# Layer ends of a five-layer graph network: unit 48 a step sooner, unit 49's kept parts ahead of the last sum, maps stored in smaller pieces

## The reference, cut to what matters

```python
edge_index = jnp.stack([src, dst])                       # dst sorted
x = _layernorm(x + _L0(x, edge_index, ...))              # sum x[src]; elu MLP 64->256->64
x = _layernorm(x + _L1(x, src, dst, edge_attr_32, ...))  # MLP per edge, sum, MLP per node
x = _layernorm(x + _L2(x, edge_index, ...))              # SAGE mean, batch norm, SAGE mean, x added
x = _layernorm(x + _L3(x, weight, src, dst, edge_type))  # x[src] @ weight[type], summed
```

## Time and profile before

| | |
|---|---|
| median of 3 runs | 9928.48 us (9926.42 to 9930.86) |
| the profiled execution's own time | 9929.83 us |
| its span, first to last instruction | 9928.0 us |
| busy share of the span | POOL 74%, PE 51%, PE weight loads 43%, DVE 26%, ACT 13% |
| gathers | 5 x 1,563 |
| mean granted TensorE clock | 0.583 of full speed |

### The profile page before, as it was taken

One profiled execution on the slowest core, in us unless ns is written; L12 is line 12 of the kernel. 1 busy time (PEld: TensorE's weight loads), 2 busy tenths in 40 slices (PEclk: granted clock), 3 DMA queues, 4 the chain that ended last, 5 costly groups with the idle time before them and its releaser, 6 DMA issues.

```text
span 9928.0 us, 68540 instructions
## 1 busy us (share of the span) xinstructions
PE 5057.8 (51%) x23622; PEld 4285.6 (43%) x23623; DVE 2602.1 (26%) x5963; ACT 1280.8 (13%) x2646; POOL 7381.4 (74%) x7823
## 2 busy tenths in 40 slices
PE   4555555566666666344444445666666633323333
PEld 3444444456666666333333334444555422222222
DVE  2222222233444443111111113333333311111111
ACT  1111111111111111000000001222222200000000
POOL 7777777767777777677777777777777667777777
PEclk6555555577777777555555555555555555555555
DMA  3111111133333333111111112222222211111111
GB/s 73 33 33 34 33 33 34 32 88 92 93 93 93 93 93 87 27 30 30 30 30 30 30 29 68 78 78 81 79 79 80 76 29 28 28 28 29 28 28 28
DMA packets 396618, 525.10 MB, mean 53 GB/s; under 512 B 175674, under 2 KB 232868, under 8 KB 396200
## 3 DMA queue, kind: packets, MB, share of 16 engines
q0 software_dynamic: 250080, 359.01, 16.0%
q1 hardware_dynamic: 56929, 81.63, 2.8%
q10 hardware_dynamic: 89255, 80.01, 2.6%
HBM read 442.81 MB, written 77.29 MB: 52 GB/s over the span
## 4 chain that ended last, share of the span: by engine, by line
POOL 74%; issue 25%; PE 1%; DVE 0%; DMA 0%; ACT 0%; ACTq 0%; POOLq 0%; DVEq 0%
POOL G L436 74%; PE PAG L1095 0%; PE NB L1095 0%; PE NA L1095 0%; PE PH L1095 0%; DMA G<-in_x,SRC 0%; DMA near_tab<-STG 0%; DVE FA L715 0%; DMA G<-rel_tab,IDX 0%; DMA h_tab<-STG 0%; ACT L503 0%; DMA G<-far_tab,SRC 0%; DMA G<-h_tab,SRC 0%; DVE HT L1031 0%; DMA G<-x_tab,SRC 0%
## 5 line engine op out<-in xcount | busy, mean ns | idle before, releaser
L1095 PE MATMUL PAG<-OH,G 128*64 128x96 f32 (+2 forms) x12544 | 2369.8, 383 | 3844.0 <-DMA G<-rel_tab,IDX 1370.1
L1095 PEld LDWEIGHTS PAG<-OH,G 128*64 128x64 f32 (+2 forms) x12544 | 2167.4, 253 | 4094.6 <-issue 3623.9
L436 POOL DMA_INDIRECT G<-rel_tab,IDX x1563 | 1474.7, 944 | 525.5 <-issue 525.5
L436 POOL DMA_INDIRECT G<-far_tab,SRC x1563 | 1474.9, 944 | 515.6 <-issue 476.1
L436 POOL DMA_INDIRECT G<-x_tab,SRC x1563 | 1475.5, 944 | 503.3 <-issue 476.0
L436 POOL DMA_INDIRECT G<-h_tab,SRC x1563 | 1475.0, 944 | 498.0 <-issue 475.7
L436 POOL DMA_INDIRECT G<-in_x,SRC x1563 | 1479.0, 946 | 476.1 <-issue 475.2
L779 DVE TENSOR_TENSOR AGG<-AGG,PAG 64x96 f32 (+2 forms) x980 | 245.6, 251 | 5510.9 <-PE PAG L1095 5501.0
L1095 PE MATMUL PAG<-OH,HT 128*128 128x96 f32 x3136 | 652.6, 393 | 630.2 <-ACT HT L614 630.2
L748 DVE TENSOR_TENSOR OH<-CONST,DREL 128x768 f32<-128x768 f32 x981 | 927.9, 946 | 3.7 <-issue 2.7
L1095 PEld LDWEIGHTS PAG<-OH,HT 128*128 128x128 f32 x3136 | 607.3, 297 | 678.0 <-ACT HT L614 677.6
(11 more groups left out here) (151 smaller groups left out, 3840.1 us busy)
## 6 DMA issues: line engine op xcount, KB each, us to landing
rel_tab<-STG ACTq DMA_DIRECT2D x100, 500.0 KB
HT<-dst_rows SPq DMA_DIRECT2D x196, 192.0 KB
HT<-in_efT SPq DMA_DIRECT2D x196, 128.0 KB
G<-in_x,SRC POOLq DMA_INDIRECT x1563
G<-far_tab,SRC POOLq DMA_INDIRECT x1563
G<-x_tab,SRC POOLq DMA_INDIRECT x1563
G<-h_tab,SRC POOLq DMA_INDIRECT x1563
G<-rel_tab,IDX POOLq DMA_INDIRECT x1563
```

What stands on the lines that cost most here:

```text
L436: pool.indirect_dma_start(out=G[:, h, j, 0:tabs[p].shape[1]], out_offset=None, in_=tabs[p], in_offset=bass.IndirectOffsetOnAxis(ap=numbers ...
L1095: return nc.tensor.matmul(dst, lhsT, rhs, start=start, stop=stop, skip_group_check=True)
```

## The change

- `SEGMENTS` and `straight_schedule`: unit 47 begins in step 188 and unit 48 in step 192, one step sooner than before; from unit 47 on a stage after the first may share a step with the stage before it. Unit 48 now ends in step 194, step 195 has no stage, and only unit 49 is left after the last step.
- `fetch` is cut in two. `keep` copies what doesn't depend on the sums (`XU`, `IU`, in layer 3 the relu of `HT`); for unit 49 it runs in step 195, ahead of the last sum. `take_sums` copies `Z` and clears `AGG`. In layer 0 `keep` also runs a one-element exp, so that the table for exp is loaded there.
- On PE the matmuls of biases and of kept parts come ahead of those that need `Z`; for unit 49 they are issued ahead of step 195's sum (`last_unit_early`). The degree goes to `PH` after the hidden products.
- The last step's sum, its mixing add and its relu and shift work on 3 chunks in place of 8.
- Layer 0's maps: the far map goes to `NA`, is copied and stored by itself and has its own semaphore, `far_stored`, for which POOL waits; the near map (with the bias) follows through `NB`. SP still waits for the near map.
- Layer 3's maps are stored in four transfers of 125 x 512 a unit in place of two of 125 x 1024.
- The one-hot matrices of the next layer's step 0 are made after unit 49; the bias row is stored without its zero half; the prologue has one more small operation (a fourth segment).

```diff
-SEGMENTS = [(0, 25, 5), (25, 40, 3), (40, UNITS - 1, 1)]
+SEGMENTS = [(0, 25, 5), (25, 40, 3), (40, UNITS - 3, 1), (UNITS - 3, UNITS - 1, 0)]
...
-            if begins[u] > s or (now and begins[u] + stage > s):
+            quick = stage > 0 and u >= SEGMENTS[-1][0]
+            if begins[u] > s or (now and begins[u] + stage - quick > s):
...
+def filled_chunks(s):
+    return max(1, min(GROUP, FILLED - s * GROUP))
...
-        STORE = [32, 16, 16, 32, 16]
+        STORE = [16, 16, 16, 64, 16]
...
                 if p == 1:
-                    pool.wait_ge(stored[0], all_stored(0))
+                    pool.wait_ge(far_stored, all_stored(0))
...
-                copy(Z[0:m, :], AGG[0:m, bass.ds(u * UNIT, UNIT)])
+            def keep(p, u):
+                if p == 0:
+                    nc.scalar.activation(WARM[:, :], ZERO[0:1, 0:1], ACT.Exp)
                 if p in (2, 3):
                     copy(IU[0:HALF, :], INV[0:HALF, bass.ds(u * 2, 2)])
...
+            def take_sums(p, u):
+                m = (D + 1, H, D, H, D)[p]
+                copy(Z[0:m, :], AGG[0:m, bass.ds(u * UNIT, UNIT)]).then_inc(staged[p], 1)
                 act.wait_ge(staged[p], u + 1)
                 act.sem_inc(act_go, 1)
                 copy(AGG[:, bass.ds(u * UNIT, UNIT)], ZERO[:, :]).then_inc(cleared[p], 1)
...
-                    act.wait_ge(l0_maps, u + 1)
-                    nc.scalar.activation(STG[0:HALF, :, 0:2 * H], NA[0:HALF, :].rearrange("p (a c) -> p a c", a=2),
-                                         ACT.Copy).then_inc(l0_maps_copied, 1)
...
+                    maps = [(l0_far, NA, 0, far_tab, far_stored), (l0_near, NB, H, near_tab, stored[0])]
+                    for k, (ready, bank, c, tab, landed) in enumerate(maps):
+                        act.wait_ge(ready, u + 1)
+                        nc.scalar.activation(STG[0:HALF, :, c:c + H],
+                                             bank[0:HALF, 0:2 * H].rearrange("p (a c) -> p a c", a=2), ACT.Copy)\
+                            .then_inc(l0_maps_copied, 1)
+                        act.wait_ge(l0_maps_copied, u * 2 + (k + 1))
+                        act.dma_start(rows_of(tab, u), STG[0:HALF, :, c:c + H]).then_inc(landed, 16)
...
+                    for k in range(4):
+                        a, b = k // 2, k % 2
+                        c = slice(b * 512, b * 512 + 512)
+                        act.wait_ge(l3_map, u * 4 + (k + 1))
+                        nc.scalar.activation(STG[0:HALF, a, c], PH[a][0:HALF, c], ACT.Copy).then_inc(l3_map_copied, 1)
+                        act.wait_ge(l3_map_copied, u * 4 + (k + 1))
+                        act.dma_start(rows_[a, b], STG[0:HALF, a, c]).then_inc(stored[3], 16)
...
+                        if s == SUPERS - 1:
+                            keep(p, LAST)
+                            if p in (1, 2):
+                                node[p](LAST, 1)
...
                     act.wait_ge(added, SUPERS * (p + 1) + 2)
-                    for u, stage in LATE:
-                        node[p](u, stage)
+                    take_sums(p, LAST)
+                    for stage in (2, 3) if p in (1, 2) else (1, 2, 3):
+                        node[p](LAST, stage)
...
-                for j in range(GROUP):
-                    last = mm(PAG[0:m, 0:WIN], msg[:, j, 0:m], OH[:, h % 2, j, :], j == 0, j == GROUP - 1)
+                for j in range(chunks):
+                    last = mm(PAG[0:m, 0:WIN], msg[:, j, 0:m], OH[:, h % 2, j, :], j == 0, j == chunks - 1)
...
+            def last_unit_early(p):
+                if p in (0, 3):
+                    node[p](LAST, 1, (0,))
+                if p in (1, 2):
+                    node[p](LAST, 1)
+                    node[p](LAST, 2, (0,))
...
+                        if s == SUPERS - 1:
+                            last_unit_early(p)
                         sum_straight(p, s, m)
-                    for u, stage in LATE:
-                        node[p](u, stage)
+                    last_unit(p)
```

More of the change, by code:

```diff
@@ L249, in gnn_kernel @@
         more_done = sem("more_done")
+        kept = [sem(f"kept{p}") for p in range(LAYERS)]
         staged = [sem(f"staged{p}") for p in range(LAYERS)]
@@ L1039, in straight @@
                     add_straight(p, SUPERS - 1, starts[SUPERS - 1], m)
-                    for u, stage in LATE:
-                        node[p](u, stage)
+                    for stage in range(4):
+                        node[p](LAST, stage)
+                    if p < LAYERS - 1:
+                        one_hot(0, DREL[:, 0, :]).then_inc(onehot_ready, 1)
                     if p == 2:
@@ L1196, in flip, with node0 @@
                 last.then_inc(flipped[p], 1)
[L1198 to L1199 removed]
+            def node0(u, stage, parts=(0, 1)):
+                if stage == 1 and 0 in parts:
+                    for a in range(2):
+                        mm(NB[0:HALF, a * D:(a + 1) * D], ONES[0:1, 0:HALF], b2r, a == 0, False)
+                if stage == 1 and 1 in parts:
                     pe.wait_ge(staged[0], u + 1)
                     for a in range(2):
[L1202 to L1203 removed]
+                        last = mm(NA[:, a * UNIT:(a + 1) * UNIT], w1[:, a * H:(a + 1) * H], Z[0:D, :])
                     last.then_inc(l0_hidden, 1)
+                    for a in range(2):
+                        last = mm(PH[0][0:HALF, a:a + 1], Z[D:D + 1, half(a)], ONES[D:D + 1, 0:1])
+                    last.then_inc(l0_degree, 1)
                 if stage == 2:
@@ L1233, in node1, with node2 @@
                     for a in range(2):
-                        last = with_bias(NB[0:HALF, a * D:(a + 1) * D], POS[:, half(a)], uw2[:, :], ub2r)
+                        last = mm(NB[0:HALF, a * D:(a + 1) * D], POS[:, half(a)], uw2[:, :], False)
                     last.then_inc(y_ready[1], 1)
-            def node2(u, stage):
+            def node2(u, stage, parts=(0, 1)):
                 if stage == 1:
-                    pe.wait_ge(staged[2], u + 1)
+                    pe.wait_ge(kept[2], u + 1)
                     flip(2, XU, D)
-                if stage == 2:
+                if stage == 2 and 0 in parts:
                     pe.wait_ge(flip_copied[2], u + 1)
@@ L1244, in node2 @@
                     for a in range(2):
-                        mm(NA[0:HALF, a * H:(a + 1) * H], Z[0:D, half(a)], wl1[:, :])
-                        last = with_bias(NB[0:HALF, a * H:(a + 1) * H], XT[0:D, half(a)], wr1[:, :], sb1r)
+                        with_bias(NB[0:HALF, a * H:(a + 1) * H], XT[0:D, half(a)], wr1[:, :], sb1r)
+                if stage == 2 and 1 in parts:
+                    pe.wait_ge(staged[2], u + 1)
+                    for a in range(2):
+                        last = mm(NA[0:HALF, a * H:(a + 1) * H], Z[0:D, half(a)], wl1[:, :])
                     last.then_inc(l2_products, 1)
@@ L1257, in batch_norm_row, with node3 @@
                 mm(NA[:, 0:H], BC[:, 2:3].to_broadcast([P, P]), IDENT[:, :]).then_inc(bn_rows, 1)
-            def node3(u, stage):
-                if stage == 1:
-                    pe.wait_ge(staged[3], u + 1)
+            def node3(u, stage, parts=(0, 1)):
+                if stage == 1 and 0 in parts:
                     pe.wait_ge(l3_hot, u + 1)
                     for a in range(2):
-                        mm(NB[0:HALF, a * D:(a + 1) * D], Z[:, half(a)], wl2[:, :])
-                        last = with_bias(NA[0:HALF, a * D:(a + 1) * D], HB[:, half(a)], wr2[:, :], sb2r)
+                        with_bias(NA[0:HALF, a * D:(a + 1) * D], HB[:, half(a)], wr2[:, :], sb2r)
+                if stage == 1 and 1 in parts:
+                    pe.wait_ge(staged[3], u + 1)
+                    for a in range(2):
+                        last = mm(NB[0:HALF, a * D:(a + 1) * D], Z[:, half(a)], wl2[:, :])
                     last.then_inc(l3_products, 1)
```

149 lines of the change are left out of this document (85 added, 64 removed).

## The result

| | before | changed |
|---|---|---|
| median of 5 runs each | 9926.85 us (9925.39 to 9930.86) | 9877.06 us (9874.48 to 9898.69) |
| ratio, 95% interval | | 0.9954 (0.9939 to 0.9968) |
| forecast | | 9880 us (9872 to 9890) |
| the profiled execution | 9929.83 us | 9898.69 us, span 9896.9 us |
| mean granted TensorE clock | 0.583 | 0.587 |

The account below looks back on a forecast made before the run. POOL's gathers were taken to bound the kernel, so only layer ends could gain: 18.9 + 9.7 + 7.4 + 10.55 + 2.25 - 0.2 = 48.6 us, from 9928.48 to 9880 us, range 9872 to 9890.

Parts of the forecast that it names:

- Layer 0: End of layer 0: earlier hidden product, less work behind it and an earlier far-map store save 18.9 us.
- The hop: From the end of a layer's last sum to the first product with `Z`: 0.87 us stays of 1.40 us.
- The exp's term: End of layer 0: loading the exp table in `keep` during step 195 takes 1.28 us off the path.
- the view that the near map is hidden: Start of layer 1: the near map lands some 2 us later, hidden by 10 us of gathers step 0 needs first.
- Layer 1: End of layer 1: product with `Z` starts 8.4 us sooner, last product without biases saves 1.25 us; 9.7 us in all.
- Layer 2: End of layer 2: product with `Z` 5.1 us sooner, products 2.3 us shorter; 7.4 us in all.
- the first rival: End of layer 1: PE, denser there, holds its full clock, 3.5 us less, 9876 us; chance 6%.
- Layer 3: End of layer 3: copies 8.75 us sooner, first transfer another 1.8 us, stretch from first issue kept at 11.1 us; 10.55 us.
- Layer 4 and prologue: After the last gather the product starts 2.25 us sooner; the start of the kernel loses 0.2 us.
- The prologue's term: Before PE's first sum: one more small VectorE operation, for which POOL waits, loses 0.2 us, between 0 and 0.4.
- The second: Layer ends 1 to 3: quarters don't overlap (3.6 us) or work before the last sum is dearer; 9884 to 9891 us; chance 13%.
- the slower one: Inside layers: gathers begin every 1.257 us instead of 1.248, giving 9,950 us; slower from 6.2 ns a gather on; chance 2%.

## Why the prediction was right

- **What bounds the kernel.** POOL's gathers do. (The 9,755 us in the forecast's text are 7,815 x 1.248; at 1.25 us they would be 9,769.) All of the gain is in the idle times between layers and behind the last gather, 49.4 us in this execution, with the first gather 0.4 us later; 48.6 were forecast. But 2.7 of the 49.4 us are the clock's, in layer 2 and behind the last gather (below), and weren't there in the profiles of chips C and D. Without them it is 46.7 us, 1.9 short of the sum: that the total fits so closely is luck.
- **Layer 0**, forecast 18.9, measured 19.4. The rows of the last gather landed after 3.20 us, not 2.5, and the sum took 1.21, not 1.05; both were under-priced, and the hidden product came 0.7 us later than forecast. The hop was 0.87 us to the digit (1980.42 to 1981.29), and the terms behind it paid 1.1 us more than I took: 0.3 in the degree products, 0.3 in the second product (1.96 us where it was 3.35), 0.2 in the far map's shorter copy, which I had left at nothing, 0.3 in the far map's issue, which had stood ahead of the near map's, and 0.1 in the store, less 0.1 in the maps. The exp's term, 1.28, was right by the run without the early exp, and so was the view that the near map is hidden.
- **Layer 1**, forecast 9.7, measured 9.9: the work between the sums took 3.45 us (3.8 forecast), the sum 1.59 (1.40).
- **Layer 2**, forecast 7.4, measured 9.3. The 1.9 us are the clock, the first rival in another layer than I had named. The stretches of the changed kernel:

```profile
5921.00:5925.00 4.00, 3.31 (x20) 3.10 (x20) 0.25 (x1) 0.24 (x1) 1.90 (x3) 0.59 0.12 25
5925.00:5929.00 4.00, 2.94 (x17) 2.27 (x18) 0.25 (x1) 0.96 (x3) 0.00 (x0) 0.83 0.01 4
```

  and its last sums of layers 2 and 4:

```profile
5926.82 0.71 PE L1141 MATMUL PAG<-OH,G 128*64 128x96 f32 x6
...
9888.63 0.68 PE L1141 MATMUL PAG<-OH,G 128*64 128x96 f32 x6 [1.43 <-DMA G<-rel_tab,IDX]
```

  The third number from the end of a stretch's row is the granted clock. In the second row it is 0.83: the 2.4 GHz level was granted for most of it, and the last sum took 0.71 us where it takes 1.22 at the 1.2 GHz level. In the run with 120 and 5 partitions, with the same order, the clock stayed at 0.50 and the idle time was 14.67 us, against 14.6 forecast. In the run with halves of 120 and 5 it rose in layer 1 instead (0.80, and 15.3 us in place of 17.3). So it comes and goes with the execution, 2 us each time. The chance of 6% that the rival had was for layer 1 alone.
- **Layer 3**, forecast 10.55, measured 7.9: here a step failed. It was "that stretch is bound by the transfer of 1,000 KB, whatever its pieces, and I keep it at 11.1 us". From the first issue it was 12.83 us. The bound by transfer was right, but the pieces weren't equal: the 2 KB packets moved more slowly on five engines (11.0 us for all of them, 9.3 for those of 4 KB), and it cost all that the earlier issue had gained. Nor was the bound the transfer of 1,000 KB as such, whatever its pieces: on fifteen engines the same bytes passed in 6.4 us. Of the other 0.9 us 0.8 are unit 48's maps, which began that much later than their twin of step 192 suggests: DVE's shift for step 194, the relu and the copy ahead of the maps stand behind the sum of step 193 (7885.23, 3.73 us).
- **Layer 4 and prologue.** Behind the last gather 2.9 us are gone against 2.25. The excess is the clock again: in the stretch 9888 to 9892 it was 0.82, and the last sum took 0.68 us, where the four variants on chips C and D took 1.19 us. There 1.8 to 2.3 us are gone. The prologue's term can't be seen, since the first gather begins at 9.4 to 10.5 us in the executions of the changed kernel and its variants and at 9.74 before.
- **The other rivals.** The second (quarters that don't overlap, or work ahead of the last sum dearer) came true in part of its size, 1.7 of 3.6 us in layer 3, but by the slower pieces and not by fixed parts that show; the clock happened to make it good. Of the slower one, the gathers' pace, the profiled execution shows 2.2 of the 6.2 ns that would have been needed, but the changed kernel itself had 944.0 ns on chip A, and the unchanged one 945.4 there and 17 us more on chip D, so the change isn't its cause. Chip A does show a slower changed kernel (ratio 1.0011), by a mechanism that I hadn't listed.

**The parts, by the runs**: unit 48 a step sooner 16.2 us, three chunks 7.4 (by durations), the far map by itself 3.1, the work ahead of the last sum 2.7, the exp table 1.3, the quarters 0. If they add, that is 30.7 of the 44.6 us between layers (46.5 less the clock's 1.9). The other 14 us weren't undone alone: the degree products and copies that left the path, and unit 48's last stage, which stays ahead of the last sum in every variant.

**What stays open**: why TensorE's sums are counted late on two of the chips, which part of the change costs layer 0 its 59 us there, and what lets the clock rise at a layer's end in one execution and not in the next. Instruction transfers are not the cause as far as the profile shows it: their number, bytes and duration are the same as in the first profiles.

## What to carry to other kernels

Where one engine paces a kernel, take its idle times at the stage changes as the whole budget, and price each from the chain behind the last piece of work; work moved from one side of the last sum to the other is worth only the wait it fills. Before a store is cut in time, see how many of the 16 transfer engines it uses: by the busy share and by the count of 4-byte packets, and choose a number of partitions with a large divisor up to 16 (120 has 15, 125 only 5), with the rest stored by itself. And compare a stretch in which nothing runs side by side when whole runs differ from chip to chip: at the end of layer 0 it repeated to 0.05 us while the total moved by 16%, but for one execution in which the clock rose and it was 0.9 us shorter. Look at the granted clock before two such stretches are compared.

## What the runs showed of the hardware that I had not expected

- The pace of the indirect gathers is a property of the execution or the chip: in layer 4 it is 1248.3 and 1248.2 ns from start to start in the first profile and with quarters of 120 and 5 partitions, 1250.4 to 1250.6 in the changed kernel's profile and in the three profiles of chip D, where the unchanged kernel took 9944.28 us in place of 9926.85. 2.2 ns a gather are 17 us, a third of what the change gives.
- What waits for TensorE's sums can be let go late, a median of 2.6 us and for a tenth of them 17 us or more behind the recorded end (0.13 us on another chip), on a chip whose other engines, transfers and granted clock (0.583 in both profiles of before) look as usual, and the same kernel then takes 11,540 us.
- A store from 125 partitions runs on 5 of the 16 transfer engines, at up to 142 GB/s; as 120 and 5 it reached 319 GB/s in its densest slice.
- The higher level of TensorE's clock was granted at a layer's end in some executions and not in others with the same order of work: 0.83 of full speed in one, 0.50 in the other, and a sum of 3 chunks took 0.71 us where it otherwise takes 1.19 to 1.22.
